# Adding an expert's rows back in counted steps of 16: a routed expert layer on eight cores

## The reference

```
Q = layernorm(x) @ Wq + bq;  K = V = Q
x = x + softmax(Q K^T / 32) V
s = sigmoid(layernorm(x) @ gate_w.T)            # 32 experts
ids = top 4 of (s + e_bias);  w = s[ids] / sum
for each expert e:  a = silu(xn @ w1[e]) * (xn @ w3[e]) * weight of e
x = x + sum over e of a @ w2[e]                 # w1, w3: 1024 x 768, w2: 768 x 1024
```

```
293 269 280 331 289 264 256 166 252 274 305 311 232 144 179 336
269 304 202 318 212 233 313 296 231 205 369 131 225 215 207 281
```

## Time and profile before

| what | value |
|---|---|
| median of 3 runs | 1684.54 us (1679.66 to 1687.63) |
| the profiled execution | 1689.26 us |
| its span on core 0, the slowest | 1687.6 us |
| spans of all cores | 1646.2 to 1687.6 us |
| PE busy on core 0 | 1253.8 us (74%) |
| Pool busy | 402.0 us (24%) |
| q0 (Pool's DMAs) | 209.69 MB, 81.0% of 16 engines |
| adds to `out` (L862) | 96, 147.4 us of Pool |

### The profile page before, as it was taken

One profiled execution on the slowest core, in us unless ns is written; L12 is line 12 of the kernel. 1 busy time (PEld: TensorE's weight loads), 2 busy tenths in 40 slices (PEclk: granted clock), 3 DMA queues, 4 the chain that ended last, 5 costly groups with the idle time before them and its releaser, 6 DMA issues.

```text
span 1687.6 us, 20536 instructions; the slowest of 8 cores (1646.2 to 1687.6 us)
## 1 busy us (share of the span) xinstructions
PE 1253.8 (74%) x7210; PEld 709.6 (42%) x7210; DVE 393.9 (23%) x846; ACT 435.6 (26%) x623; POOL 402.0 (24%) x377
## 2 busy tenths in 40 slices
PE   3989899888637966666866696676759766677797
PEld 1545455555324533333433353343435433344453
DVE  3624444444431111111111121111111111111121
ACT  3743323333212211211312121121212211122231
POOL 0000222211132222221422222242222222233222
PEclk8999989888867977988988798888879888888898
DMA  7999999611052999999999999999999999999953
GB/s 168 216 189 129 143 127 138 123 54 63 38 175 55 167 167 193 166 163 188 167 166 169 183 163 174 184 171 167 171 180 167 172 175 185 172 166 168 168 107 57
DMA packets 109222, 257.18 MB, mean 152 GB/s; under 512 B 11352, under 2 KB 11736, under 8 KB 107584
## 3 DMA queue, kind: packets, MB, share of 16 engines
q0 software_dynamic: 96512, 209.69, 81.0%
q1 hardware_dynamic: 12464, 46.14, 9.3%
q10 hardware_dynamic: 144, 0.03, 0.0%
HBM read 364.94 MB, written 68.19 MB: 257 GB/s over the span
## 4 chain that ended last, share of the span: by engine, by line
DMA 50%; PE 28%; issue 5%; DVE 5%; POOL 5%; ACT 3%; another core or an unknown queue 2%; POOLq 1%; DVEq 0%; ACTq 0%; SPq 0%
DMA out<-yb,t_meta 36%; DMA xg<-xnd,t_meta 11%; PE pss L807 8%; PE pav L489 6%; PE pav L838 4%; PE pss L449 4%; POOL out L862 3%; PE ptr L540 3%; PE ptr L320 2%; PE pss L367 1%; DMA wq<-wqd 1%; ACT xn L565 1%; DMA xb<-xd 1%; POOL xg L776 1%
## 5 line engine op out<-in xcount | busy, mean ns | idle before, releaser
L807 PE MATMUL pss<-xgt,wp 128*128 128x384 bf16 x2016 | 339.4, 328 | 1.4 <-ACT xgt L794 1.4
L320 PE MATMUL ptr<-c_idb,xg 128*128 128x128 bf16 x768 | 81.9, 284 | 324.8 <-DMA xg<-xnd,t_meta 308.4
L807 PEld LDWEIGHTS pss<-xgt,wp 128*128 128x128 bf16 x2016 | 198.2, 98 | 135.9 <-issue 4.8
L862 POOL DMA_INDIRECT out<-yb,t_meta x96 | 147.4, 1536 | 285.6 <-DMA out<-yb,t_meta 208.9
L320 PEld LDWEIGHTS ptr<-c_idb,xg 128*128 128x128 bf16 x768 | 68.4, 129 | 341.9 <-issue 341.5
L821 DVE TENSOR_TENSOR at<-sil,pss 128x384 bf16<-128x384 bf16 x192 | 106.5, 555 | 452.2 <-PE pss L807 452.2
L847 DVE TENSOR_SCALAR yb<-pav,t_meta 128x512 f32<-128x512 f32 x96 | 72.1, 751 | 547.6 <-PE pav L838 542.7
L794 ACT COPY xgt<-ptr 128x1024 bf16<-128x1024 bf16 x96 | 97.3, 1013 | 373.9 <-PE ptr L320 364.8
L818 ACT ACTIVATE sil<-pss 128x384 bf16<-128x384 f32 x192 | 94.5, 492 | 358.4 <-PE pss L807 358.4
L838 PE MATMUL pav<-wp,at 128*128 128x512 bf16 x756 | 179.6, 398 | 0.1
L807 PE MATMUL pss<-xgt,wr 128*128 128x384 bf16 x1056 | 178.8, 326 | 0.0
(11 more groups left out here) (100 smaller groups left out, 781.9 us busy)
## 6 DMA issues: line engine op xcount, KB each, us to landing
wp<-w1d POOLq DMA_DIRECT2D x21, 1536.0 KB, 35.1
wp<-w3d POOLq DMA_DIRECT2D x21, 1536.0 KB, 27.6
wp<-w2d POOLq DMA_DIRECT2D x17, 1536.0 KB, 26.4
xb<-xd SPq DMA_DIRECT2D x32, 512.0 KB, 9.4
wr<-w1d POOLq DMA_DIRECT2D x10, 1536.0 KB, 40.7
wr<-w3d POOLq DMA_DIRECT2D x9, 1536.0 KB, 37.5
wr<-w2d POOLq DMA_DIRECT2D x8, 1536.0 KB, 31.7
wcd<-w2d POOLq DMA_DIRECT2D x7, 1536.0 KB
```

Of the source, the lines that this page charges most:

```text
L320: ins = e.transpose(dst[:, k * 128:(k + 1) * 128], src_of(k), ident)
L807: ins = e.matmul(pss[:, bnk * 512:bnk * 512 + CAP], unit_ap(u, c * ID + ic * 128, 128), xgt[:, xo + c * CAP:xo + (c + 1) * CAP], start=(c ...
L862: return e.indirect_dma_start(out=outd[:, :], out_offset=bass.IndirectOffsetOnAxis(ap=t_meta[0:n, 2 * c:2 * c + 1], axis=0), in_=yb[0:n, y ...
```

## The change

The third block's four cases become eight, and the second block is counted as well. `pick` halves the interval from 16 to 128 rows by branches, three deep, until one number of rows is left; that is the smallest multiple of 16 that holds the expert's rows in this block, and 16 where it has none. The first block stays at 128 rows. Each counted block loads the register itself.

```diff
-                def add_last_rows(e, done, b=b, add_rows=add_rows):
-
+                def add_counted_rows(e, done, b=b, add_rows=add_rows):
+
+                    def pick(lo, hi):
+                        if lo == hi:
+                            done(add_rows(e, lo))
+                            return
+                        mid = (lo + hi) // 32 * 16
+                        with e.If_lt(cnt_reg, b * 128 + mid + 1):
+                            pick(lo, mid)
+                        with e.Else():
+                            pick(mid + 16, hi)
                     e.reg_load(cnt_reg, t_cnt[0:1, ei:ei + 1])
-                    with e.If_lt(cnt_reg, b * 128 + 33):
-                        done(add_rows(e, 32))
-                    with e.Else():
-                        with e.If_lt(cnt_reg, b * 128 + 65):
-                            done(add_rows(e, 64))
-                        with e.Else():
-                            with e.If_lt(cnt_reg, b * 128 + 97):
-                                done(add_rows(e, 96))
-                            with e.Else():
-                                done(add_rows(e, 128))
+                    pick(16, 128)
 
                 waits = [*ye_tok[(ei, b)], *prev]
-                if b < NB - 1:
+                if b == 0:
                     y_sc[ei] = p.d(lambda e, add_rows=add_rows: add_rows(e, 128), "dY", *waits,
                                    eng="gpsimd")
                 else:
-                    y_sc[ei] = p.put("gpsimd", add_last_rows, [*waits, v_cnt], "dY", 16,
+                    y_sc[ei] = p.put("gpsimd", add_counted_rows, [*waits, v_cnt], "dY", 16,
                                      branches=True)
```

## The result

The changed kernel takes 1672.07 us (median of 20 runs) against 1688.22 us of the kernel before (20 runs): ratio 0.9893, 95% interval 0.9868 to 0.9917, so 18.1 us less (14.0 to 22.3). The ratio and its interval leave out the runs in which the cores of one die ran at a lower clock; the two medians hold all 20. The forecast was a ratio of 1667.0/1684.5 = 0.9896. The profiled execution took 1670.05 us, its slowest core is now core 1.

The account below looks back on a forecast made before the run. The prediction took the total work of Pool's DMA queue to bound the experts' stretch; 752 rows at 23.2 ns (-17.4 us) plus 0.3 us of branches gave -17.1 us, from 1684.5 to 1667 us, range 1655 to 1677.

Parts of the forecast that it names:

- The bound: Experts' stretch, 560 to 1589 us: bound by the total work of Pool's DMA queue, share 1.05, while PE waits.
- Where it ends: At 1589 us, PE's last late gather (expert 29); rows of experts 27 to 31 are worth nothing but at the very end.
- A sign that can't be read: Test stated ahead: the prediction is wrong if the time before the experts moves.
- The number of rows: Adds on core 0: 1024 of 9696 rows go, 752 of them in experts 0 to 26.
- The price of a row: Adds in the experts' stretch: 24.4 ns alone, 23.2 ns of wall time at share 1.05; 752 rows give 17.4 us.
- Rival 2: Adds in the experts' stretch: a row costs only a packet, 12.9 ns, or part is lost; 1675 us, chance 0.17.
- rival 3: Experts' stretch: adds slow the weights as well, a row up to 44.6 ns; down to 1651 us, chance 0.13.
- The sum: Whole kernel: -17.4 us for rows and +0.3 us for the last add's branches, -17.1 us, to 1667 us.
- core 0 stays last: Other cores lose 672 to 752 rows in the first part; core 3, 4 us below, loses 720.
- The trees: Branches on Pool's sequencer before each counted add: hidden behind the add before, no cost in the stage, 0.3 us at the end.
- Rival 4: Adds in the experts' stretch: short adds spread badly, so adds with fewer rows land no earlier; chance not given.
- Rival 5: Pool's counted adds: branch trees stall its instruction supply; 1721 us at 22 us a stall, chance 0.05.

Follow-up runs that it names:

- The step with the largest dose: All three blocks add 128 rows, with no count and no branch, against the kernel before: ratio 1.0358 (1.0318 to 1.0398), +60 us.

## Why the prediction was right

**The bound.** Right (but the earlier trace rows has PE at 5 to 9 over the experts, and DMA at 5 and 3 in the last two slices, not 6 to 8 and 9 throughout). In every window shown the share stayed at 1.05 or 1.06, with rows taken out, 2072 rows put in, or the reads of 7230 rows left out, and in the large steps the time followed the rows. In the finest ones (steps of 8: 202 rows, -1.7 us of the stretch) that can't be seen.

**Where it ends.** Right: rows of experts 27 to 31 gave 1.0007, and PE again waits once (11.5 us on core 1), and then no more.

**A sign that can't be read.** The prediction called itself wrong if the time before the experts moved. On core 0 it did, by 17.8 us, with nothing changed there; the mean of the eight cores moved by 2.2 us (553.9 to 551.7). One execution on one core can't carry that test.

**The number of rows.** Right to one step of 16 on core 0 (1040 packets for 1024).

**The price of a row.** Taken as 23.2 ns from an add alone in the queue, and this term of the sum was too small. The step with the largest dose measured 27.4 ns in the stretch and 28.4 (25.2 to 31.6) by the ratio; the other stretches gave 27 to 32. Rival 2 is out: its 12.9 ns lie far below the 25.2 at which the interval begins, and the read of the old row costs as much by itself (12.8). The far end of rival 3, 44.6, is out too. Where the missing 4 ns or more come from is not shown. Rival 3, the adds' traffic slowing the weights, could give them, but GB/s did not rise with the rows gone (174 on core 1 before and after), and nothing shows that the read costs more in the crowd than alone. The sample was the other weak spot: one core's adds of one expert, nearly all with 128 rows, while adds alone took 27.6 to 28.7 ns a row in the three executions of the changed kernel. A price of 27 to 29 can be had from these without any crowd; no run separates the two.

**The sum.** -17.1 us was forecast, 18.1 measured (14.0 to 22.3). At 27.4 ns the 752 rows would be 20.6 us, less the end. That 18.1 came out nearer to 17 has room in the interval, and is in part luck: the price was too small, and the slowest core gained less than the mean one (the mean stretch alone, which leaves out expert 0, fell by 21.4 us). The slowest core is also not always core 0. The step "core 0 stays last" failed: in the profiled execution core 1 is last, with 688 rows in the stretch, and cores shift by tens of us from run to run. By the rows this error is small, because all cores lose 672 to 752 of them; what the shifts between cores do to the total is not shown.

**The trees.** Right: 1.001. The cover named (Pool's work on the add before, and the queue's stock) holds. At the end of the kernel, where there is none, the trees cost: in the profiles the last three adds span 5.70 us where they spanned 5.48, and from the last one to the end it is 9.65 us where it was 9.26 (means of the cores). 0.6 us together, 0.3 were forecast. The kernel with the trees and the rows of before has the same 5.70 and 9.62, so it is the trees.

**Rival 4**, bad spread, did not happen: the shapes 48, 80 and 112 are in the change, and even shapes like 24 and 40 cost nothing that shows. **Rival 5**, stalls: gaps of 0.27 to 0.31 us between the adds of every expert up to 26 on every core.

## What to carry to other kernels

Here the DMA queue had a share of 1.05 and the engines waited for it, and a row of padding cost its own time wherever in that stretch it stood. Price such a row by the same transfer alone in a quiet stretch, but take transfers of several lengths and on several cores: one sample said 23.2 ns, the stage 27 to 32. The branches on the issuing engine (0.04 us and some 0.1 of issue each) cost nothing that shows while it was busy with the transfer before. Find first where the bound ends: the same rows behind that point were worth nothing.

## What was not expected

- Nearly half of the price of a row added by DMA is the read of the old row, with the adding: 12.8 of 27.4 ns (of 32 on its own chip), 92.6 us of this kernel's stretch. That is more than the counted rows bring, so a way that needs fewer reads of old rows would be worth a look; none was tried.
- Adds of odd multiples of 8 rows did no harm that shows, in a kernel that makes some 25 of them per core before the bound ends.
- Single cores differ between executions by tens of us (core 0: 1628 to 1676 us), much of it ahead of the experts. The fall of 40.5 us on core 0 in the profiles is more than twice what the change gives.
